# Products of a narrow chunk ahead of the wait for the next diagonals, in a two-layer graph attention kernel

## The reference

```python
# layer 0 (slope 0.2, values are the entity embeddings)
scores = (x @ W @ a1)[:, None] + (E @ W @ a2)[None, :]
e = where(scores > 0, scores, 0.2 * scores)
attention = softmax(where(adj > 0, e, -9e15), axis=1)
x = layernorm(x + elu(attention @ E + x))
# layer 1 (slope 0.01, values are wh)
wh = x @ W1
e = leaky_relu((wh @ a_src)[:, None] + (wh @ a_dst)[None, :], 0.01)
attention = softmax(where(adj > 0, e, -1e9), axis=1)
x = layernorm(x + attention @ wh + bias)
```

## Time and profile before

| quantity | value |
|---|---|
| median of three runs | 645.31 us |
| profiled execution, whole | 640.76 us |
| profiled execution, span of its instructions | 639.0 us |
| TensorE matmul busy | 507.5 us, 79% of the span |
| VectorE busy | 558.4 us, 87% |
| ScalarE busy | 536.6 us, 84% |
| GpSimd busy | 178.6 us, 28% |
| mean granted TensorE clock | 0.963 of full speed |

### The profile page before, as it was taken

One profiled execution on the slowest core, in us unless ns is written; L12 is line 12 of the kernel. 1 busy time (PEld: TensorE's weight loads), 2 busy tenths in 40 slices (PEclk: granted clock), 3 DMA queues, 4 the chain that ended last, 5 costly groups with the idle time before them and its releaser, 6 DMA issues.

```text
span 639.0 us, 14279 instructions
## 1 busy us (share of the span) xinstructions
PE 507.5 (79%) x6039; PEld 236.9 (37%) x6039; DVE 558.4 (87%) x758; ACT 536.6 (84%) x618; POOL 178.6 (28%) x116
## 2 busy tenths in 40 slices
PE   1308776989989799999989785668889888899994
PEld 1204444434444234433445442333333333333452
DVE  2899999999889998989769888869997999899795
ACT  0878995989999998899989878648998899789883
POOL 2240100276026650287001057005301340121050
PEclk9999789889999999999989989879999899999997
DMA  9898985767567745550100100000001000000000
GB/s 219 354 368 297 345 325 189 249 223 257 185 235 273 235 162 232 184 172 2 34 18 2 35 3 1 35 0 1 10 2 34 1 17 1 18 2 17 1 16 12
DMA packets 18252, 76.16 MB, mean 119 GB/s; under 512 B 6300, under 2 KB 8524, under 8 KB 9996
## 3 DMA queue, kind: packets, MB, share of 16 engines
q1 hardware_dynamic: 17304, 74.87, 33.8%
q0 software_dynamic: 112, 0.28, 0.2%
q10 hardware_dynamic: 772, 0.10, 0.1%
HBM read 74.16 MB, written 1.09 MB: 118 GB/s over the span
## 4 chain that ended last, share of the span: by engine, by line
issue 29%; DVE 25%; ACT 20%; PE 18%; POOL 4%; DMA 3%; ACTq 1%; POOLq 0%; DVEq 0%
ACT Pm L786 15%; DVE junk L906 13%; PE acc L1172 9%; PE zps L1227 5%; DVE zps L1054 5%; DMA adj_in<-in_adj 3%; DVE v L883 2%; ACT zps L778 2%; PE acc L1179 1%; ACT v L646 1%; DMA acol<-in_L_gnn_weight_a 1%; POOL rstd L590 1%; PE zps L1142 1%; ACT u_row L662 1%; DVE D L926 1%
## 5 line engine op out<-in xcount | busy, mean ns | idle before, releaser
L786 ACT ACTIVATE Pm<-zps,ebias 128x1024 f32<-128x1024 f32 (+1 forms) x320 | 292.0, 934 | 55.3 <-DVE zps L1054 43.5
L1227 PE MATMUL zps<-D,v 128*128 128x128 bf16 x2048 | 166.4, 226 | 54.6 <-DVE D L926 32.3
L778 ACT ACTIVATE zps<-S_row,ntau_col 128x1024 f32<-128x1024 f32 (+1 forms) x203 | 195.1, 963 | 5.4
L1227 PEld LDWEIGHTS zps<-D,v 128*128 128x128 fp8e4 x2048 | 120.3, 100 | 195.7 <-ACT zps L778 82.9
L1172 PE MATMUL acc<-Pm,VE 128*32 128x512 f32 (+2 forms) x1280 | 149.1, 539 | 17.5 <-ACT Pm L786 12.7
L1172 PE MATMUL acc<-Pm,X 128*32 128x512 f32 (+2 forms) x1280 | 141.4, 531 | 23.5 <-ACT Pm L786 21.9
L1054 DVE SCALAR_TENSOR_TENSOR zps<-S_row,tau_col,zps 128x1024 f32<-128x1024 f32 (+1 forms) x117 | 118.4, 1034 | 43.7 <-PE zps L1227 42.9
L906 DVE CUSTOM_DVE_ANT_0 junk<-v,adj_in 128x2048 int8<-128x2048 int8 (+3 forms) x80 | 154.6, 1959 | 1.7 <-ACT adj_in L667 1.7
L906 DVE CUSTOM_DVE_ANT_0 junk<-v,u_row 128x2048 int8<-128x2048 int8 x64 | 155.4, 2444 | 0.2
L1179 PE MATMUL acc<-Pm,ones 128*32 128x256 f32 (+1 forms) x1280 | 87.6, 347 | 0.0
L521 POOL TENSOR_TENSOR tAB<-flag,totW 128x520 f32<-128x520 f32 (+1 forms) x8 | 10.6, 1329 | 252.7 <-issue 163.5
(11 more groups left out here) (163 smaller groups left out, 257.5 us busy)
## 6 DMA issues: line engine op xcount, KB each, us to landing
adj_in<-in_adj SPq DMA_DIRECT2D x62, 1024.0 KB, 6.2
S_row<-S_rows_scratch SPq DMA_DIRECT2D x6, 512.0 KB, 3.9
Pm<-in_adj SPq DMA_DIRECT2D x2, 1024.0 KB, 5.7
S_row<-S_rows_scratch SPq DMA_DIRECT2D x3, 256.0 KB, 3.2
out<-tAB SPq DMA_DIRECT2D x3, 256.0 KB, 2.7
adj_in<-u_row_scratch SPq DMA_DIRECT2D x2, 256.0 KB, 3.2
S_row<-S_rows_scratch POOLq DMA_DIRECT2D x1, 256.0 KB, 7.4
out<-tAB SPq DMA_DIRECT2D x2, 128.0 KB, 2.3
```

Source lines behind the costliest of these rows:

```text
L778: a.activation(mask_of(n), S_row[:, C % 2, 0:R(C) * P], ACT.Relu, bias=ntau_col[:, layer(C), n % JT:n % JT + 1]).then_inc(seed_done, 1)
L786: a.activation(Pm_of(k, 0, R(C) * P), mask_of(k), ACT.Exp, bias=ebias[:, layer(C), int(seeded(k)), J:J + 1])\
L1227: last = t.matmul(mask[:, r * P:(r + 1) * P], v[:, chunks[C][1] + r, J * P:(J + 1) * P], D[:, C % 2, PART * second + r, :], start=(r * P % ...
```

## The change

There are two edits. In the loop of TensorE, the products that a narrow chunk has left are put ahead of the wait for the next chunk's diagonals; this concerns the ends of chunks 0, 4 and 5. In `diagonals` of VectorE, the writing of the diagonals is put ahead of the flags (or, for chunk 5, of the two copies); this concerns chunks 0 to 9.

```diff
@@ def diagonals(C)
                     dve.wait_ge(turned, JT * (C - 1))
                 if C - 2 in SPREAD:
                     dve.wait_ge(uspread_done, JT // GT + C - 2 - SPREAD[0] + 1)
+                write_diagonals(C, 0)
                 if C == NC:
                     link(d.tensor_copy(um_known[:, :], um8[:, 0:PART]))
                     d.tensor_copy(g_parts[:, 0, :], g8[:, 0:PART])
                 else:
                     write_flags(C, um8[:, 0:R(C)])
-                write_diagonals(C, 0)
@@ loop of TensorE
             for C in range(NCH):
+
+                while C and narrow(C - 1) and next_product < JT * C:
+                    product(next_product)
+                    next_product += 1
                 pe.wait_ge(D_ready, diagonals_of(C))
                 for J in range(JT):
                     k = JT * C + J
```

## The result

| | before | after |
|---|---|---|
| first timing, median of 7 runs each | 642.08 us (640.63 to 646.23) | 637.69 us (635.80 to 640.49) |
| ratio, with 95% interval | | 0.9912 [0.9884, 0.9940] |
| profiled execution | 640.76 us | 637.38 us |
| its span | 639.0 us | 635.6 us |
| mean granted clock | 0.963 | 0.968 |

By the ratio the change makes the kernel 0.9% faster, about 5.7 us; the two medians lie 4.4 us apart. The forecast was 4.2 us less, from 645.31 to 641.1. The gain in size was nearly met, and the level from which it was taken was not: the median of the kernel before, taken at 645.31 from three runs, is 642.08 over seven, and 642.8 to 644.6 over the 11 to 26 runs of the later comparisons.

A forecast was written before the change was run, and what follows sets the result against it. No engine alone was taken to bound the kernel, but the hand-overs between engines at chunk heads. Gains of 0.45 + 1.05 + 2.50 + 0.20 = 4.2 us took 645.31 to 641.1 us, range 636.5 to 646.0.

The forecast's parts named there:

- the last of the sum: Whole kernel: the 4.2 us gain is taken from the three-run median of 645.31, not the profiled 640.76, giving 641.1.
- Head of chunk 1, term 0.45: Products just fit before the diagonals, so VectorE's second L1054 starts earlier: 0.45 us gained, bounds -0.2 and 1.0.
- Head of chunk 5, term 1.05: Products delay the first mask step, but the accumulator's save and the projection come earlier: 1.05 us gained, bounds -0.55 and 1.12.
- rival 2: Slack takes up the small gains at chunks 1 and 5, there through GpSimd's chain: 642.6 us, chance 0.15.
- Head of chunk 6, term 2.50: At full clock the save no longer waits and the first product starts 2.50 us earlier, bounds 0.3 and 2.5.
- Chunk 9 and the other chunks: Earlier diagonals gain 0.2 us at chunk 9 (bounds 0 and 0.21) and nothing at chunks 2, 3, 4, 7 and 8.
- rival 1: The clock at chunk 6 still falls, leaving 0.3 to 1.5 us there and about 2.6 in all: 642.7 us, chance 0.15.
- rival 3: Early products leave longer holes: 3.4 us lost to low clock at chunk 1, chunk 6's 2.5 gone: 647.0 us, chance 0.07.

The follow-up runs named there:

- warm5b: The changed kernel with mask step 2 of chunk 5 done eight times and 30 unused matmuls behind its mask step 4: 635.27 us, one profile.
- heads16: The changed kernel with products put ahead at chunks 1 and 6 only, chunk 5 in the old order: 637.02 us over four runs, ratio 0.989.
- the repeat: The changed kernel measured and profiled once more without an edit: 637.60 us, ratio 0.990 to the kernel before.
- warm6_only: The kernel before with 72 unused matmuls put ahead of the wait for chunk 6's diagonals: 642.22 us, ratio 0.998.
- before_third: The kernel before, profiled a third time without an edit: 645.43 us.
- only_tensor: The changed kernel with the diagonals put back behind flags and copies, so TensorE's edit alone: 639.21 us, ratio 0.9931.
- warm5: The changed kernel with mask step 2 of chunk 5 done eight times: 638.36 us over four runs, ratio 0.990.
- warm_all: As warm5, with 48 unused matmuls ahead of chunk 4's score rows and 36 ahead of chunk 6's diagonals: 638.06 us, ratio 0.990.

## Why the prediction was right and wrong

**The step that failed is the last of the sum**, "I carry the difference over: 645.31 - 4.2 = 641.1". It took the median of three runs as the level, though its own text said that these differ by 3.2 us and that the profile lay 4.55 below. Over 7 runs the level is 642.08, so of the 3.4 us by which the forecast missed 637.69, 3.2 are the level. Against that level a time of 641.1 would be hardly any change, while 4.4 us less (by the medians) or 5.7 (by the ratio) was measured. That 642.08 - 4.2 lies so near the measured time is in part luck, for the terms of the sum are off in both directions, as told below.

The scatter of the old kernel is in large part its clock. In the three later comparisons it ran 54 times. All 27 runs over 644 us had a mean granted clock of 0.961 or less, and 22 of the 27 under 644 had 0.962 or more. The three profiles agree: the execution in which chunks 1, 5 and 8 were slowed by the clock took 645.4, those in which they were not, or less, 640.8 and 641.0. I had both numbers and no mechanism for their distance.

**Head of chunk 1, term 0.45.** Right in its working: at the same clock 0.42, with the second L1054 0.4 us earlier against the linked term. It is the term that is most mis-sized as a gain: over seven and six profiles 1.7, of which 0.6 may be chance. I cited the 3.07 us hole at 101 as proof that such a hole keeps the clock; it had kept it in that run. In three of the six profiles with the old order the clock fell at this head (at 101.3, 101.8 and 102.6 us), and chunk 1 took 74.1 to 74.3. In the new order it never took over 72.44. The term left out what the three products between the mask steps cost at half clock, 1.5 to 1.7 us at the second L1054.

**Head of chunk 5, term 1.05.** Right for the first steps and at full clock, and gone by step 6 in the change as it stands. VectorE's first maxima of the chunk start 3.72 us behind the linked term instead of 4.85, the 1.1 forecast. Then the clock fell 4.8 us behind the linked term in the new order and 10.9 behind it in the old, and by step 6 the gain was 0.06. At full clock the order gives 0.87 there and 0.72 at the chunk's end (`warm5b` to `heads16`), so rival 2 (slack in GpSimd's chain) is wrong as a mechanism. The means give 1.0, with an interval that holds 0, and the shortest chunk 5 without fillings, 42.12, has the old order. Whether this head gives anything in the change as it stands is not shown.

**Head of chunk 6, term 2.50.** To 0.01 in the first pair, with the clock full as I took it. That was in part luck: "With 2.8 us of idle time I take the full clock" held for mask step 0 in four of six profiles, and only in the first was the clock full through the whole head; in the other five it was at half for some of the 10 us behind the linked term. In the repeat the hole was the same, and the three mask steps took 2.74 us instead of 1.51:

```profile
418.09 2.74 PE L1231 MATMUL zps<-D,v 128*128 128x128 bf16 x24 [2.73 <-DVE D L926]
```

Over all profiles the term is 1.7. Its split was wrong: I had 0.4 for mask step 0 at the low clock and took the rest for order, when the three products behind it at half clock cost 1 us more (`warm6_only`: 1.46 for the clock alone).

**Chunk 9 and the other chunks.** 0.2 at the tail, as forecast; nothing at chunks 2, 3, 4, 7 and 8. Missed was chunk 0, whose diagonals are written by the same function: 0.2 to 0.3 at the start, where I had written that the change does not touch it.

**Rivals.** The clock was the right rival and the wrong sign. I let it take from the gain (rival 1) or cost a low stretch more (rival 3); at chunk 1 it adds in the mean, for three profiles with the old order had a fall on the path of VectorE's first steps and none with the new one. Rival 1 came true in part: at chunk 6 the mean gain is 0.8 us under the term. Rival 3 names what happens at chunk 5, longer holes behind work done early, but it costs 1.2 us there and not 3.4. At chunk 1 the low stretch behind mask step 4 was no longer than before, 3.4 us in both.

**What stays open.** The places add up to 4.8 us, the timings to 5.7 and 6.4. Two of three profiles of before lie at 640.8 and 641.0, below its medians, so the means of the old order are probably still too low. Chunk 8, 57.1 or 58.5 in kernels of both orders, is the clock again: the four profiles with 58.5 (`before_third`, `only_tensor`, `heads16`, `warm5`) are at half clock 16 to 20 us behind its linked term, and the ten with 57.1 have no fall in it. Why the clock falls there in some executions is open.

## What to carry to other kernels

Where an engine waits with finished work in hand, do that work first: it pays what it moves off the path, and it can pay again when that engine is running slowly. Then look at the next hole of that engine, where its clock may fall earlier than it did. Before a small gain is forecast, find out why the runs of the old kernel differ, by profiling it two or three times; one profile is one draw, and its span can't be laid on a median. For a stage in which TensorE has holes, price its steps at half clock as well as at full.

## What the runs showed of the hardware

The granted clock fell to 1.2 GHz at other places in each execution of the same program, also behind the same hole: 3.07 us of idle time ahead of chunk 1 left it full, 3.64 us, in another execution, were followed by a fall within the first product. Ahead of chunk 6, 2.72 us left it full in the change and 2.73 in the repeat did not, so the length of the hole alone doesn't tell. Chunks 1, 5 and 6 have a length that depends on it (1 to 3 us), in some executions chunks 4 and 8 too; chunks 2, 3 and 7 repeat to 0.08 us. The Trainium skill says of the clock (TensorE: Matmul & The Clock Gate, What's actually happening) that activity releases a throttle that is there by default; the fillings agree, as 58 more matmuls, none of which the result needs, in two holes of chunk 5 made it 1.2 us shorter.

A filled hole can move the fall to the next one (`warm5`, `warm_all`) rather than take it away; in chunk 5 only closing both holes was worth anything, while in chunk 6 of the kernel before one filled hole gave 1.2 to 1.5 us (`warm6_only`).
